# Reordering P's transposes, the value product's waits and hw's bank in a fused attention and feed-forward kernel

## What is computed

```python
# x: (128, 32, 512); cond: (128, 128)
x = x + attention(cond_mix(x, cond))       # per-sequence 32x32 mixing, then 32 query heads, 8 kv heads, causal softmax, Wo
x = x + lora_moe(grouped_conv(x, cond))    # 9-tap conv, base linear plus 8 LoRA experts, weighted by a router
# attention:  q, k, v = y @ Wq, y @ Wk, y @ Wv ; rope(q), rope(k)
#             P = softmax(q k^T / 4, causal) ; (P v) @ Wo
# lora_moe:   z @ base_W.T + base_b + 2 * sum_e w_e * ((z @ A_e.T) @ B_e.T)      ("hw" below is h * w)
```

## Time and profile before

| | |
|---|---|
| median of 3 runs | 609.29 us (609.05 to 610.1) |
| the profiled execution | 612.12 us |
| its span in the trace | 610.3 us |
| around the span | 1.8 us |
| PE busy | 586.5 us (96%) |
| DVE busy | 494.5 us (81%) |
| ACT, POOL busy | 36%, 37% |
| mean granted TensorE clock | 0.992 |

### The profile page before, as it was taken

One profiled execution on the slowest core, in us unless ns is written; L12 is line 12 of the kernel. 1 busy time (PEld: TensorE's weight loads), 2 busy tenths in 40 slices (PEclk: granted clock), 3 DMA queues, 4 the chain that ended last, 5 costly groups with the idle time before them and its releaser, 6 DMA issues.

```text
span 610.3 us, 14252 instructions
## 1 busy us (share of the span) xinstructions
PE 586.5 (96%) x4937; PEld 493.8 (81%) x4937; DVE 494.5 (81%) x1236; ACT 221.4 (36%) x603; POOL 225.9 (37%) x182
## 2 busy tenths in 40 slices
PE   5789999999999999999999999999999999999986
PEld 4577888888889888888888888888888888898864
DVE  4658788888888888888888888888888888888855
ACT  4344333333333333334333433333333334334321
POOL 7344244333333433233344333343443333334310
PEclk9879999999999999999999999999999999999999
DMA  8547553445555434455553345455534455554241
GB/s 186 109 145 158 117 130 107 94 113 112 116 133 133 116 96 111 99 112 133 133 133 109 90 111 111 113 133 133 129 101 97 107 117 117 133 133 112 64 112 59
DMA packets 122086, 71.26 MB, mean 117 GB/s; under 512 B 45661, under 2 KB 104189, under 8 KB 121944
## 3 DMA queue, kind: packets, MB, share of 16 engines
q1 hardware_dynamic: 120576, 70.53, 48.7%
q0 software_dynamic: 144, 0.28, 0.3%
q10 hardware_dynamic: 1352, 0.27, 0.2%
HBM read 51.53 MB, written 19.53 MB: 116 GB/s over the span
## 4 chain that ended last, share of the span: by engine, by line
PE 78%; DMA 10%; DVE 5%; SPq 3%; issue 2%; ACT 1%; ACTq 1%; DVEq 0%
PE ps L435 17%; PE ps L602 15%; PE ps L623 9%; DMA scratch<-x_dram 6%; PE ps L629 5%; PE ps L665 5%; PE ps L539 4%; PE ps L657 4%; PE ps L684 3%; PE ps L706 3%; PE ps L576 3%; PE ps L673 2%; PE ps L613 2%; PE ps L579 2%; DVE x1p L1290 1%
## 5 line engine op out<-in xcount | busy, mean ns | idle before, releaser
L1013 POOL TENSOR_TENSOR qk<-network,t 128x640 f32<-128x640 f32 x31 | 48.3, 1558 | 162.6 <-DVE t L1206 162.6
L435 PE MATMUL ps<-wqkv_hi,y_hi 128*128 128x512 f32 (+1 forms) x256 | 87.8, 343 | 0.9 <-POOL y_lo L1003 0.5
L435 PE MATMUL ps<-wqkv_lo,y_hi 128*128 128x512 f32 (+1 forms) x256 | 87.4, 342 | 0.0
L435 PE MATMUL ps<-wqkv_hi,y_lo 128*128 128x512 f32 (+1 forms) x256 | 87.4, 342 | 0.0
L1025 POOL TENSOR_TENSOR raw<-x1p,basebB 128x512 f32<-128x512 f32 x32 | 49.5, 1547 | 57.8 <-DVE x1p L1290 57.6
L799 ACT ACTIVATE raw<-ps 128x512 f32<-128x512 f32 x64 | 37.7, 595 | 76.0 <-PE ps L684 75.9
L1020 POOL TENSOR_TENSOR raw<-raw,zero 128x512 f32<-128x512 f32 x32 | 33.3, 1040 | 73.9 <-DVE raw L1279 73.9
L435 PEld LDWEIGHTS ps<-wqkv_hi,y_hi 128*128 128x128 f32 x256 | 48.8, 191 | 8.8 <-ACT y_hi L799 2.0
L997 POOL TENSOR_TENSOR raw<-raw,rz 128x512 f32<-128x512 f32 x32 | 33.6, 1049 | 59.4 <-DVE rz L1235 59.4
L435 PEld LDWEIGHTS ps<-wqkv_lo,y_hi 128*128 128x128 f32 x256 | 48.9, 191 | 6.1
L435 PEld LDWEIGHTS ps<-wqkv_hi,y_lo 128*128 128x128 f32 x256 | 48.8, 191 | 6.0
(11 more groups left out here) (204 smaller groups left out, 1468.9 us busy)
## 6 DMA issues: line engine op xcount, KB each, us to landing
scratch<-x_dram SPq DMA_DIRECT2D x96, 256.0 KB, 5.8
x_dram<-x1p SPq DMA_DIRECT2D x32, 260.0 KB, 2.0
xm<-x SPq DMA_DIRECT2D x32, 256.0 KB, 4.4
xr<-x SPq DMA_DIRECT2D x32, 256.0 KB, 2.7
out<-raw SPq DMA_DIRECT2D x32, 256.0 KB, 2.1
v_dram<-vS SPq DMA_DIRECT2D x32, 64.0 KB
vB<-v_dram SPq DMA_DIRECT2D x128, 16.0 KB, 4.8
mixb<-mixb_dram SPq DMA_DIRECT2D x28, 64.0 KB, 3.9
```

Of the source, the lines that this page charges most:

```text
L435: last = mm(dst, a, b, start=(n == 0), stop=(n == 3 * len(left) - 1))
L1013: nc.gpsimd.tensor_tensor(qk[:, :], t1, t2[:, :], ALU.add).then_inc(qk_sb, 1)
```

## The change

Five edits. Peeled steps keep most of the old order.

- For t = 3 to 30 `keys_values(t + 1)` runs behind `transpose_p(t)` instead of ahead of it.
- The waits for vB_in and pT_sb move out of `values` into `values_ready`, which stands ahead of `conv(t - 1)` (behind it in t = 1; t = 31 unchanged in place).
- hw's transpose goes to bank 3 instead of bank 7, except for the last three groups; the wait for hwT_lo_sb ahead of `values` goes.
- The product of two columns (L700) goes.
- ScalarE copies both halves of P ahead of the high part of hw's transpose.

```diff
+        def hwT_bank(u):
+            return 7 if isinstance(u, int) and u >= G - 3 else 3
+        def keys_late(t):
+            return not isinstance(t, int) or 3 <= t < G - 1

+            def values_ready(t):
+                pe.wait_ge(vB_in, 16 * HK * (t + 1))
+                pe.wait_ge(pT_sb, 2 * t + 2)
             def values(t):
-                pe.wait_ge(vB_in, 16 * HK * (t + 1))
-                if live(t - 2) and not peeled(t, G - 1):
-                    pe.wait_ge(hwT_lo_sb, t - 1)
                 ...
-                pe.wait_ge(pT_sb, 2 * t + 2)
-                if not isinstance(t, int):
-                    mm(ps[0:S, 4, 0:2], convW[:, 0, :, :].rearrange("p j o -> p (j o)"), xc[:, 0, 0:2], start=True, stop=True)

             def transpose_hw(u):
-                nc.tensor.transpose(ps[:, 7, 0:P], hw...).then_inc(hwT_ps, 1)
+                nc.tensor.transpose(ps[:, hwT_bank(u), 0:P], hw...).then_inc(hwT_ps, 1)

 # TensorE, steps(t)
                 if live(t + 1):
                     queries(t + 1)
+                if live(t + 1) and not keys_late(t):
                     keys_values(t + 1)
                 ...
                 if live(t):
                     transpose_p(t)
+                if live(t + 1) and keys_late(t):
+                    keys_values(t + 1)
                 if peeled(t, G - 1):
+                    values_ready(t)
                     values(t)
                 ...
+                if live(t) and not peeled(t, G - 1):
+                    if not peeled(t, 1):
+                        values_ready(t)
                 if live(t - 1) and not peeled(t, G):
                     conv(t - 1)
+                if peeled(t, 1):
+                    values_ready(t)
                 if live(t) and not peeled(t, G - 1):
                     values(t)

 # ScalarE, steps(t)
                 if live(t):
                     transposed_p(t, 0)
-                if live(t) and peeled(t, G - 1):
+                if live(t):
                     transposed_p(t, 1)
                 if live(t - 2) and not peeled(t, G - 1):
                     high_hwT(t)
-                if live(t) and not peeled(t, G - 1):
-                    transposed_p(t, 1)
```

More of the change, by code:

```diff
@@ L712, in transpose_hw @@
                 pe.wait_ge(hw_sb, u + 1)
-                nc.tensor.transpose(ps[:, 7, 0:P], hw[:, :, :].rearrange("p e r -> p (e r)"), ident).then_inc(hwT_ps, 1)
+                nc.tensor.transpose(ps[:, hwT_bank(u), 0:P], hw[:, :, :].rearrange("p e r -> p (e r)"), ident).then_inc(hwT_ps, 1)
             def steps(t):
@@ L885, in high_hwT @@
                 act.wait_ge(hwT_ps, t - 1)
-                copy(hwT_hi[:, :], ps[:, 7, 0:P]).then_inc(hwT_hi_sb, 1)
+                copy(hwT_hi[:, :], ps[:, hwT_bank(t - 2), 0:P]).then_inc(hwT_hi_sb, 1)
             def next_y_hi(u):
@@ L1252, in low_hwT @@
                 dve.wait_ge(hwT_hi_sb, t - 1)
-                minus(hwT_lo[:, :], ps[:, 7, 0:P], hwT_hi[:, :]).then_inc(hwT_lo_sb, 1)
+                minus(hwT_lo[:, :], ps[:, hwT_bank(t - 2), 0:P], hwT_hi[:, :]).then_inc(hwT_lo_sb, 1)
             def low_oT(t):
```

## The result

The changed kernel takes 624.04 us (median of 4 runs, 620.97 to 626.67) where the kernel before took 609.32 us (609.05 to 610.1): a ratio of 1.024 with a 95% interval of 1.018 to 1.029, so it is 14.7 us slower. The forecast was slower by 7 us, with a range that ended at 619 us.

A forecast was written before the change was run, and what follows sets the result against it. TensorE's order plus its real waits was taken to bound the 17.53 us loop step. 26 x (0.47 - 0.20) = 7.0 us, with +0.5, -0.2, -0.1 and +0.1, gave +7.3 us: 616 us, range 607.5 to 619.

The forecast's parts named there:

- vB lands behind the convolution's start, and the wait is paid anew in each step: Ahead of the convolution, t = 4 to 29: vB's fourth transfer lands 0.41 us (mean) after its start, delaying every step 0.47 us.
- 0.06 us from landing to start: Ahead of the convolution on TensorE: it was taken to start 0.06 us after the last awaited transfer lands.
- Convolution to value product 0.93 us, between 0.85 and 1.00: On TensorE: this distance falls from 1.127 us to the middle of two bounds, gaining 0.20 us a step (0.13 to 0.28).
- The two-column product costs 0.15 us: Between convolution and value product: the small product was read to cost 0.15 us more in an ordinary step.
- The landing would keep its distance to the projection: In SyncE's transfers: from the previous step's projection to vB's landing the distance stays, even when the convolution starts later.
- The added change between plain fp32 and fp32r, 0 to 0.11 us: On TensorE, keys and values behind P's transposes: one more type change a step, mostly hidden in the wait, +0.1 us in all.
- P ready in time for its early transposes: Ahead of P's transposes: P is needed 1.4 us sooner, with 1.1 us of slack left, so cost 0.
- rival 3: P's transposes wait for VectorE because P isn't ready, adding to the vB wait: over 619 us, chance 0.02.
- Rivals 1 and 2: vB lands sooner unprofiled: by 0.37 us, 608.5 to 610.5 us, chance 0.13; by over 0.4 us, 604.3 to 606.5 us, chance 0.13.
- rival 1: Transfers a little faster without the profiler, so gain and wait cancel: 608.5 to 610.5 us, chance 0.13.
- the restart: Ahead of the convolution on TensorE: the time from vB's landing to the convolution's start, taken as 0.06 us.

## Why the prediction was right or wrong

The direction, the mechanism and its place held; the size did not: +14.7 us against +7.3. By its own steps:

- **vB lands behind the convolution's start, and the wait is paid anew in each step: right.** The wait moved alone costs 8 to 10 us, and put back it costs nothing. The lateness itself was read rightly: 16.84 us from value product to landing before, 16.81 to 16.82 us in three of the variants.
- **0.06 us from landing to start: wrong, the largest error.** It was read from starts behind the convolution's own wait, with nothing between that wait and the convolution. The change put two more waits behind the vB wait, and the traces show 0.06 to 0.10 us for each such wait. Measured 0.205 us, so 26 x 0.145 = 3.8 us were missing by the traces. The variant with the vB wait last has 0.036 us and is faster than the changed kernel, 620.18 us (ratio 1.013) against 624.04 (1.024).
- **Convolution to value product 0.93 us, between 0.85 and 1.00: wrong choice, as the upper bound was the value.** It is 1.00 to 1.01 us (medians) in every kernel in which nothing else held it. The product of the convolution's own tile shape was the wrong neighbour; the whole-array product at 1.00 us was the right one. That is 26 x 0.08 = 2.1 us.
- The rule of the Trainium skill (TensorEngine Tiling (Array Packing), Key Properties), by which a change of tiling mode drains TensorE, has no time with it but pointed at the whole-array neighbour. The traces agree: 1.00 us to either other tile shape, 0.85 us to the same.
- **The two-column product costs 0.15 us: wrong, it costs 0.02 us.** Its gain was inside the same term: of the 0.15 us of waiting for ScalarE and the 0.15 us of the product only the first could be won.
- **The landing would keep its distance to the projection: nearly right.** It came 0.08 us later in the mean, 26 x 0.08 = 2.0 us, through a few late steps. Some 1.2 us of that is the stretch at the lower granted clock, told above; the rest is open.
- **The added change between plain fp32 and fp32r, 0 to 0.11 us: it is 0 to 0.02.** P's transposes, keys and values take 310.83 - 308.55 = 2.28 us in the new order; the same 20 products took 303.87 - 301.60 = 2.27 us in the old one.
- **P ready in time for its early transposes: right.** They show no wait, and rival 3 falls.
- **Rivals 1 and 2, landings sooner without the profiler: wrong.** The timed runs lost as much as the traced ones. The 2.8 us between profile and median that rival 1 leaned on go with the granted clock, 0.992 in that profile: the kernel before took 608.4 to 611.8 us in 27 of 28 runs at 0.994 or more, and 613.1 to 616.7 us in the 8 runs at 0.992 or less. But what they say the edits would gain without the wait was right: 2.8 to 5 us, and with SyncE's order the same on both sides it is 4 us.

3.8 + 2.1 + 2.0 us on top of 7.3 make 15.2 us, against 14.7 measured. So the steps that failed are three terms of the sum, the restart first. The range ended too low because its upper end took the distance from convolution to value product at its bound of 1.00 us, but kept the restart at one value, 0.06 us, read where no wait stood in between, and the landing at its old place. The advice of the Trainium skill (DMA: Bandwidth & Descriptors, Rules for kernel authors), to wait late, is borne out by both variants that move this one wait: 8 to 10 us lost in one, the whole loss won back in the other.

## What to carry to other kernels

Before a wait is moved ahead of a piece of work, read when what it waits for lands against the start of that work, not against its end: here the convolution's 1.1 us were all that hid transfers that land 0.4 us into it. Where several waits stand in a row, put the one that ends last in the last place. And where a transfer is late, look first at the issues ahead of it in its queue: moving loads that nothing used for another 10 us cost nothing. Where TensorE waited for vB, in the changed kernel, it was worth 20 us; in the kernel before, where it didn't, nothing that could be measured.

## What the runs showed of the hardware

- A wait that is already satisfied isn't free behind one that ends late: 0.04, 0.11, 0.21 and 0.33 us from landing to start with 0, 1, 2 and 4 such waits in between, after 0.14 us of idle time as after 1.83 us. Ahead of the last one they are hidden (0.04 us with both moved there).
- After four products on 96 x 32 tiles the next product starts 1.00 us behind their start on 64 x 32 tiles as on the whole array, and 0.85 us behind it on the same tile shape; a small product of the same shape in between adds 0.02 us.
- The three transfers of the convolution took 5.8 us to landing (median) with three other loads issued just ahead of them, and 4.0 to 4.1 us without.
- SyncE's own issues get slower in a busy queue: from the first to the fourth vB issue it took 2.39 us (mean) with those loads ahead and 1.91 us without.
- The granted clock goes with the spread: 608.4 to 611.8 us for the kernel before at 0.994 or more (one run 613.7), 613.1 to 616.7 us at 0.992 or less.
- In one step the granted clock fell to 0.50 just after TensorE had waited 1.83 us; after a wait of 1.89 us in another trace it stayed at 1.00.
